# A transformer block of eight sequences: the hand-written step orders of five stages are replaced

## The reference

```python
x = layernorm(x + attention(x))      # 16 heads of 16, Wqkv, bqkv, Wo, bo
x = layernorm(x + ffn(x))            # expert width 1024
```

## Time and profile before

| | |
|---|---|
| median of 3 runs | 621.63 us (621.22 to 622.06) |
| profiled execution, its span | 619.31 us |
| TensorE matmul, busy | 583.6 us, 94% |
| VectorE, busy | 494.4 us, 80% |
| ScalarE, busy | 318.8 us, 51% |
| GpSimd, busy | 299.0 us, 48% |
| mean share of the DMA engines | 37.5% |

### The profile page before, as it was taken

How to read it: one execution, slowest core, us unless ns; L and a number is a source line. 1 busy time by engine, 2 the same in 40 slices (tenths; PEclk the granted TensorE clock), 3 DMA queues, 4 the chain that set the end, 5 groups by cost and what they waited for, 6 DMA issues and landing times.

```text
span 619.3 us, 12888 instructions
## 1 busy us (share of the span) xinstructions
PE 583.6 (94%) x4012; PEld 342.5 (55%) x4012; DVE 494.4 (80%) x1258; ACT 318.8 (51%) x593; POOL 299.0 (48%) x504
## 2 busy tenths in 40 slices
PE   5789888999999999999999999999999999999995
PEld 3344354664656555674556646575556646446674
DVE  5388968996799868989599877989599877993766
ACT  2129713459247644477246653476345753576262
POOL 1306695346275535465174543654264452654234
PEclk9789998999999999999999999999999999999998
DMA  6965715005462073502653064601644054600101
GB/s 158 289 175 206 211 51 161 23 29 163 122 172 66 3 229 115 166 1 83 161 166 100 1 199 123 160 28 52 186 144 127 1 166 105 206 2 3 35 1 35
DMA packets 47724, 68.49 MB, mean 111 GB/s; under 512 B 4857, under 2 KB 43641, under 8 KB 44793
## 3 DMA queue, kind: packets, MB, share of 16 engines
q1 hardware_dynamic: 47691, 68.08, 37.5%
HBM read 38.44 MB, written 29.36 MB: 109 GB/s over the span
## 4 chain that ended last, share of the span: by engine, by line
PE 78%; DVE 5%; ACT 5%; POOL 5%; issue 4%; DMA 2%; SPq 0%; POOLq 0%; DVEq 0%
PE ring L698 17%; PE max_bank L613 10%; PE acc L647 9%; PE ring L635 9%; PE ring L590 8%; PE acc L715 7%; PE ring L597 4%; ACT probs L772 4%; PE ring L671 4%; PE max_bank L618 2%; PE ring L655 2%; POOL probs L1042 2%; PE ring L684 1%; POOL tern_down L1085 1%; PE max_bank L715 1%
## 5 line engine op out<-in xcount | busy, mean ns | idle before, releaser
L772 ACT ACTIVATE probs<-ring 128x512 f32<-128x512 f32 x320 | 170.7, 606 | 45.6 <-PE ring L635 44.0
L1042 POOL TENSOR_SCALAR_AFFINE_SELECT probs<-probs 128x256 f32<-128x256 f32 (+1 forms) x320 | 120.5, 401 | 130.1 <-ACT probs L772 129.4
L896 DVE CUSTOM_DVE_ANT_0 max_bank<-max_bank,causal_wide 128x384 f32<-128x384 f32 (+1 forms) x256 | 157.2, 637 | 15.3 <-PE max_bank L613 12.2
L613 PE MATMUL max_bank<-k_stack,q_stack 112*128 112x384 bf16 (+3 forms) x512 | 123.4, 304 | 5.9 <-DVE neg_max L896 2.8
L1078 POOL TENSOR_TENSOR hidden_lo<-hidden,hidden_hi 128x512 f16<-128x512 f32 (+1 forms) x72 | 75.1, 1050 | 63.6 <-ACT hidden_hi L803 63.3
L635 PE MATMUL ring<-q_stack,k_stack 114*128 114x512 bf16 (+3 forms) x512 | 103.7, 300 | 1.6 <-DVE attn L921 0.5
L791 ACT ACTIVATE gating<-ring,tanh_scale 128x512 f32<-128x512 f32 (+1 forms) x72 | 45.8, 639 | 74.0 <-PE ring L698 74.0
L647 PE MATMUL acc<-probs,v_ones 128*32 128x512 f32 (+3 forms) x1024 | 79.9, 437 | 2.8 <-POOL probs L1042 2.8
L613 PEld LDWEIGHTS max_bank<-k_stack,q_stack 112*128 112x128 bf16 x512 | 46.5, 98 | 54.0 <-DVE neg_max L896 15.3
L900 DVE TENSOR_REDUCE neg_max<-max_bank 128x2 f32<-128x512 f32 (+1 forms) x96 | 63.7, 686 | 10.4 <-PE max_bank L618 8.7
L635 PEld LDWEIGHTS ring<-q_stack,k_stack 114*128 114x128 bf16 x512 | 44.5, 97 | 49.4 <-issue 17.0
(11 more groups left out here) (107 smaller groups left out, 866.0 us busy)
## 6 DMA issues: line engine op xcount, KB each, us to landing
q_stack<-qk_scratch SPq DMA_DIRECT2D x15, 768.0 KB, 6.1
k_stack<-k_slots SPq DMA_DIRECT2D x15, 768.0 KB, 7.8
qk_scratch<-qk_parts SPq DMA_DIRECT2D x16, 384.0 KB, 3.0
k_slots<-qk_parts SPq DMA_DIRECT2D x16, 384.0 KB, 2.6
xin<-x_dram SPq DMA_DIRECT2D x8, 512.0 KB, 3.5
qk_scratch<-qk_parts SPq DMA_DIRECT2D x16, 256.0 KB, 3.2
k_slots<-qk_parts SPq DMA_DIRECT2D x16, 256.0 KB, 2.3
res<-x_dram SPq DMA_DIRECT2D x8, 512.0 KB, 3.4
```

The source lines that it names most:

```text
L613: mm = pe.matmul(max_bank[k][:, width * i:width * (i + 1)], q_stack[0:MAX_ROW, 4 * g + h, P * tile:P * (tile + 1)], k_stack[0:MAX_ROW, 4 * ...
L772: rg.drained(act.activation(probs[:, g % 2, n, :], rg.bank(step)[:, :], ACT.Exp), step)
L896: dve.tensor_tensor_reduce(scores, scores, causal_wide[:, SEQ - width:SEQ], -1.0, LOWEST_START, ALU.add, ALU.min, neg_max[:, g, first_col: ...
L1042: return pool.affine_select(out=v, in_=v, compare_op=ALU.is_ge, fill=0.0, base=0, pattern=([[0, blocks]] if blocks > 1 else []) + [[1, P]] ...
```

## The change

The order strings of FIRST, SECOND, LOOP, SEVENTH and LAST are written anew; PRE's is as it was. Every string holds the same steps as before (217, 261, 261, 245 and 110), so no operation is added, removed or given to another engine. The wait that VectorE did in SEVENTH before overwriting `z` is now done in every stage but FIRST.

What moves, in the main:

- LOOP, TensorE: the front was qk.2, max.0.0, max.0.1, qk.3, v.0, max.0.2, x1t.0, ... and is v.0, max.0.0, v.1, max.0.1, qk.2, qk.3, max.0.2, max.0.3, x1t.0, ... The up and gate steps come earlier in part; qk.0 and qk.1 come one exp later each at the end.
- LOOP, VectorE: ln2 goes from behind mt_out.3 to directly in front of wo.0.1; nt_out.1 from before split.1 to behind the copy of pv.2.3; ffn_stats.1 behind mt_out.3; ln1 behind take.0.0.
- LOOP, GpSimd and SyncE: on GpSimd load_res's four additions go from before split.2 to behind hidden_hi.2. On SyncE load_next and load_res go in front of part_write.3.2 and stack_read.1, and store from before part_write.0.1 to behind stack_read.0. 
- SECOND: four v and qk.2, qk.3 in front of x1t.0 (before: three v, both qk); ln1 behind take.0.9 (before: take.0.7); ln2 at the end as in LOOP; load_next first and load_res in the middle.
- SEVENTH: v.1 and qk.3 come in front of x1t.0, pv and exp steps earlier, load_res late, and the store before the last pv steps.
- FIRST: v.0 in front of qk.3, wsum behind exp.2.6 (before: exp.3.3), qk.0 before max.3.0 and ternary.1 in front of the copy of pv.2.3, nt_out.1 behind it; at.0 between pv.3.0 and pv.3.1.
- LAST: another order in the middle; gate.7.1 before down.2.1, ln2.0 before ffn_sum.1.

```diff
--- before.py
+++ after.py
...
 FIRST_ORDER = """
-    qk.2 qk.3 part_write.2.0 v.0 split.2 max.0.0 max.0.1 max.0.2 max.0.3 max.0.4 max.0.5 max.0.6 part_write.3.0
-    take.0.0 max.0.7 max.0.8 take.0.1 take.0.2 max.0.9 take.0.3 take.0.4 v.1 max.0.10 max.1.0 take.0.5 take.0.6
...
-    pv.1.1 nt.0 exp.2.6 take.3.10 mt.3 qk.1 exp.2.7 split.0 exp.2.8 mt_out.3 exp.2.9 pv.1.2 nt_out.0 pv.1.3 exp.3.0
-    exp.3.1 part_write.0.1 exp.3.2 exp.3.3 qk_out.1 nt.1 split.1 wsum exp.3.4 exp.3.5 exp.3.6 exp.3.7 nt_out.1
-    exp.3.8 pv.2.0 exp.3.9 pv.2.1 ternary.0 ternary.2.0 pv.2.2 pv.2.3 nt.2 ternary.2.1 pv.3.0 part_write.0.2 pv.3.1
-    pv.3.2 part_write.1.0 ternary.1 part_write.1.1 part_write.1.2 nt_out.2 pv.3.3 at.0 ternary.2.2 nt.3 nt_out.3
-    wo.0.0 wo.1.0 at.1 wo.0.1 stack_read.0 wo.1.1
+    split.2 take.0.0 qk.2 v.0 take.0.1 qk.3 max.0.0 v.1 take.0.2 max.0.1 take.0.3 take.0.4 max.0.2 max.0.3 max.0.4
+    max.0.5 max.0.6 max.0.7 max.0.8 split.3 take.0.5 take.0.6 part_write.2.0 part_write.2.1 take.0.7 max.0.9
...
+    exp.2.5 split.0 take.3.10 nt_out.0 mt.3 exp.2.6 mt_out.3 wsum part_write.1.0 exp.2.7 part_write.1.1 exp.2.8
+    pv.1.2 part_write.1.2 exp.2.9 ternary.0 qk.1 exp.3.0 part_write.0.2 pv.1.3 exp.3.1 exp.3.2 exp.3.3 exp.3.4
+    exp.3.5 exp.3.6 nt.1 exp.3.7 stack_read.0 qk_out.1 exp.3.8 split.1 pv.2.0 exp.3.9 pv.2.1 ternary.2.0 pv.2.2
+    ternary.2.1 ternary.1 pv.2.3 nt.2 pv.3.0 at.0 nt_out.1 pv.3.1 nt_out.2 pv.3.2 pv.3.3 wo.0.0 nt.3 nt_out.3 at.1
+    wo.1.0 wo.0.1 wo.1.1 ternary.2.2
...
 SECOND_ORDER = """
-    max.0.0 v.0 max.0.1 v_out.0 qk.2 take.0.0 max.0.2 max.0.3 take.0.1 take.0.2 max.0.4 max.0.5 v.1 take.0.3 max.0.6
-    take.0.4 take.0.5 take.0.6 max.0.7 qk.3 v.2 take.0.7 ln1 max.0.8 v_out.1 max.0.9 load_next x1t.0 x1t.1 take.0.8
-    split.2 x1_lo.0 max.0.10 x1_lo.1 take.0.9 v_out.2 up.0 part_write.2.0 up.1 part_write.2.1 max.1.0 gate.0
...
-    ffn_stats.0 exp.3.0 exp.3.1 ffn_stats.1 exp.3.2 exp.3.3 pv.2.0 exp.3.4 exp.3.5 nt_out.0 exp.3.6 exp.3.7 exp.3.8
-    pv.2.1 pv.2.2 pv.2.3 exp.3.9 nt.1 ln2 nt.2 nt_out.1 pv.3.0 load_res pv.3.1 pv.3.2 part_write.1.2 nt_out.2 pv.3.3
-    at.0 nt.3 wo.0.0 nt_out.3 at.1 stack_read.0 store wo.1.0 wo.0.1 wo.1.1
+    take.0.0 load_next take.0.1 max.0.0 max.0.1 qk.2 v.0 v.1 take.0.2 v.2 v_out.0 take.0.3 v_out.1 take.0.4 max.0.2
+    max.0.3 v_out.2 take.0.5 take.0.6 take.0.7 v_out.3 max.0.4 take.0.8 max.0.5 take.0.9 max.0.6 ln1 take.0.10
+    max.0.7 max.0.8 take.1.0 x1_lo.0 max.0.9 v.3 qk.3 max.0.10 max.1.0 x1t.0 x1t.1 part_write.3.0 max.1.1 x1_lo.1
...
+    ffn_stats.0 exp.3.4 pv.2.0 exp.3.5 exp.3.6 part_write.1.0 nt_out.0 split.1 exp.3.7 exp.3.8 part_write.0.2 pv.2.1
+    pv.2.2 pv.2.3 nt_out.1 exp.3.9 part_write.1.1 part_write.1.2 nt.1 nt.2 nt_out.2 pv.3.0 pv.3.1 pv.3.2
+    stack_read.0 store ffn_stats.1 pv.3.3 at.0 nt.3 nt_out.3 wo.0.0 at.1 ln2 wo.1.0 wo.0.1 wo.1.1
...
 LOOP_ORDER = """
-    qk.2 max.0.0 max.0.1 take.0.0 qk.3 take.0.1 v.0 max.0.2 ln1 x1t.0 max.0.3 x1t.1 max.0.4 v.1 v_out.0 take.0.2
-    load_res take.0.3 max.0.5 v.2 part_write.3.0 max.0.6 max.0.7 x1_lo.0 take.0.4 take.0.5 part_write.2.0 x1_lo.1
-    v_out.1 v_out.2 split.2 up.0 take.0.6 take.0.7 gate.0 swish.0 max.0.8 up.1 swiglu.0 split.3 take.0.8
...
-    max.1.7 down.1 swiglu.3 v.3 take.1.5 hidden_hi.3 swiglu.4 max.1.8 max.1.9 v_out.3 gate.5 take.1.6 hidden_hi.4
-    part_write.3.2 up.6 max.1.10 stack_read.1 take.1.7 up.7 max.2.0 mt_out.0 exp.0.0 swish.5 take.1.8 max.2.1
-    swiglu.5 load_next down.2 take.1.9 max.2.2 take.1.10 exp.0.1 swish.6 max.2.3 take.2.0 take.2.1 exp.0.2 swish.7
...
-    mt_out.3 qk.0 exp.2.8 nt.0 ln2 exp.2.9 qk_out.0 pv.1.2 part_write.0.0 pv.1.3 nt_out.0 exp.3.0 exp.3.1 store
-    split.0 exp.3.2 qk.1 exp.3.3 part_write.0.1 exp.3.4 nt.1 exp.3.5 qk_out.1 exp.3.6 exp.3.7 exp.3.8 nt_out.1
-    exp.3.9 pv.2.0 split.1 pv.2.1 pv.2.2 pv.2.3 pv.3.0 nt.2 part_write.1.0 part_write.0.2 pv.3.1 pv.3.2
-    part_write.1.1 nt_out.2 pv.3.3 at.0 nt.3 nt_out.3 part_write.1.2 wo.0.0 at.1 wo.1.0 wo.0.1 wo.1.1 stack_read.0
+    take.0.0 v.0 v_out.0 ln1 max.0.0 v.1 split.2 part_write.3.0 v_out.1 part_write.2.0 take.0.1 take.0.2
+    part_write.2.1 max.0.1 take.0.3 qk.2 qk.3 take.0.4 x1_lo.0 x1_lo.1 max.0.2 max.0.3 x1t.0 max.0.4 take.0.5
+    take.0.6 swish.0 take.0.7 swiglu.0 part_write.2.2 x1t.1 v_out.2 max.0.5 swish.1 v.2 take.0.8 split.3 max.0.6
...
+    down.1 mt.0 hidden_hi.1 v_out.3 max.1.5 gate.4 swish.3 max.1.6 max.1.7 hidden_hi.2 take.1.1 swiglu.2 up.5
+    max.1.8 gate.5 load_res max.1.9 hidden_hi.3 up.6 swish.4 part_write.3.2 stack_read.1 max.1.10 take.1.2 down.2
...
+    nt.0 ffn_stats.1 exp.2.8 nt_out.0 qk.0 exp.2.9 pv.1.2 exp.3.0 pv.1.3 exp.3.1 qk_out.0 exp.3.2 exp.3.3 qk.1
+    part_write.0.0 exp.3.4 exp.3.5 split.0 qk_out.1 part_write.0.1 exp.3.6 exp.3.7 exp.3.8 nt.1 exp.3.9 split.1
+    pv.2.0 part_write.0.2 part_write.1.0 pv.2.1 pv.2.2 part_write.1.1 pv.2.3 nt_out.1 pv.3.0 nt.2 pv.3.1 pv.3.2
+    part_write.1.2 nt_out.2 pv.3.3 nt_out.3 at.0 ln2 stack_read.0 nt.3 wo.0.0 at.1 wo.1.0 wo.0.1 wo.1.1 store
...
 SEVENTH_ORDER = """
-    qk.2 max.0.0 max.0.1 v.0 v_out.0 max.0.2 take.0.0 take.0.1 max.0.3 ln1 load_res take.0.2 x1t.0 v.1 split.2
-    max.0.4 x1t.1 max.0.5 v_out.1 take.0.3 x1_lo.0 qk.3 take.0.4 part_write.3.0 max.0.6 take.0.5 max.0.7 x1_lo.1 v.2
...
-    ffn_stats.0 ffn_sum.1 pv.2.3 pv.3.0 ffn_stats.1 pv.3.1 pv.3.2 pv.3.3 nt.2 nt_out.2 nt.3 at.0 nt_out.3 at.1 ln2
-    wo.0.0 wo.0.1 store wo.1.0 wo.1.1
+    take.0.0 part_write.3.0 v_out.0 part_write.2.0 take.0.1 qk.2 max.0.0 part_write.2.1 max.0.1 v.0 ln1 take.0.2
+    v_out.1 v.1 take.0.3 take.0.4 max.0.2 max.0.3 take.0.5 qk.3 part_write.2.2 max.0.4 take.0.6 x1_lo.0 x1t.0
+    max.0.5 max.0.6 x1_lo.1 x1t.1 max.0.7 take.0.7 take.0.8 split.2 part_write.3.1 v.2 v_out.2 max.0.8 take.0.9 up.0
...
+    exp.3.9 pv.2.0 pv.2.1 ffn_stats.1 pv.2.2 pv.2.3 pv.3.0 pv.3.1 pv.3.2 pv.3.3 nt_out.2 nt.2 nt.3 at.0 nt_out.3 ln2
+    at.1 wo.0.0 wo.0.1 wo.1.0 wo.1.1
...
 LAST_ORDER = """
-    ln1.0 x1t.0 x1_lo.0 up.0.0 swish.0.0 up.1.0 swish.1.0 gate.0.0 up.2.0 ln1.1 swiglu.0.0 swish.2.0 gate.1.0
...
-    swiglu.7.1 down.5.1 down.6.1 hidden_hi.7.1 down.7.1 ffn_sum.1 ffn_stats.1 ln2.0 ln2.1 store.0 store.1
+    x1t.0 ln1.0 x1_lo.0 up.0.0 swish.0.0 gate.0.0 swiglu.0.0 swish.1.0 swiglu.1.0 swish.2.0 swish.3.0 up.1.0
...
+    swiglu.7.1 gate.7.1 down.2.1 ln2.0 down.3.1 down.4.1 down.5.1 ffn_sum.1 ffn_stats.1 down.6.1 ln2.1 down.7.1
...
@@ -927,8 +927,8 @@
                         u = step[1]
                         bank = ("wo", u, 0)
                         if u == 0:
-                            if name == "SEVENTH":
-                                dve.wait_ge(y_done, TT * b)
+                            if not first:
+                                at_least(dve, y_done, TT, b, 0)
                                 dve.sem_inc(dve_passed, 1)
                             at_least(dve, res_biased, 1, b, 1)
                         rg.wait_filled(dve, bank)
```

116 lines of the change are left out of this document (58 added, 58 removed).

## The result

The changed kernel took 632.75 us (median of 4 runs, 630.98 to 633.23), the kernel before 621.73 us (4 runs, 621.22 to 622.06). The ratio is 1.0183, with a 95% interval of 1.0163 to 1.0204: the change made the kernel 11 us slower. The profiled execution spans 631.40 us, 12.1 more than that of before.

The account below looks back on a forecast made before the run. TensorE, busy 94% of the span, was taken as the bound. Terms -0.5 - 2.0 - 2.0 - 1.4 - 0.4 = -6.3 us took the span from 619.31 to 613.0; adding 2.32 gave 615.3, range 609 to 624.

Parts of the forecast that it names:

- What changes is cover: All stages: a new order changes only the TensorE work standing between a chain's start and the step needing its end.
- 5 x -0.4: LOOP's term: five iterations each 0.4 us shorter, -2.0 us in all; bounds per iteration -0.7 and +1.0.
- The 0.4 us goes: LOOP: with qk.1 one exp later, pv.3.0's 0.4 us wait for GpSimd's mask disappears.
- The sums of TensorE's work up to pv.2.0 and behind it come out the same.: LOOP: the new order leaves TensorE's total work on either side of pv.2.0 unchanged.
- The slack that I summed: LOOP: least slack of VectorE's takes against TensorE's max steps, first 10 us, goes from -0.2 to +0.3.
- -2.0: SECOND's term: x1t wait -1.5, takes -0.4, slow clock -0.1; bounds -4 and +3.5 us.
- the second rival: LOOP stays and var_eps meets GpSimd's step, making SECOND +1.0 instead of -2.0: 620.3 us; chance 0.20.
- -1.4: SEVENTH's term: more TensorE work ahead of x1t.0 removes the 1.37 us lost there; bounds +0.5 and -2.5.
- tight place further on: SEVENTH's upper bound: another tight place later in the stage could make it 0.5 us longer.
- -0.5: FIRST's term: copy 2.3 us later, way behind it 2.0 shorter, 0.8 of VectorE's front idle gone; bounds -5.5, +8.
- The third's event: FIRST: GpSimd takes the port first and holds VectorE's ternary.1 for 5.4 to 10.8 us; middle 623.4, chance 0.15.
- The first's: FIRST pays in full, 5.5 us gained instead of 0.5, total 610.3 us; chance 0.13.

Follow-up runs that it names:

- c3: Kernel before with GpSimd's third down-weight instruction moved behind split.3 in SECOND, and LOOP's nt.1, nt_out.1, ln2 and store moved as in the change: 616.93 us, ratio 0.9933.
- b2: Changed kernel with FIRST as before, SECOND's qk.3 behind v.2, LOOP's nt.1 and nt_out.1 earlier, SEVENTH's down.3 ahead of exp.3.0: 629.23 us, ratio 1.0118.
- b1: Kernel before with SECOND as changed but qk.3 behind v.2, and LOOP's qk.0 and qk.1 one exp later each: 624.86 us, ratio 1.0051.
- a2: Changed kernel with LOOP's pv.1.0 put directly ahead of pv.1.1 and pv.1.2 directly ahead of pv.1.3: 635.57 us, ratio 1.0206.
- b3: Changed kernel with FIRST's ternary.1 behind the copy and nt_out.1 ahead, LOOP's pv groups joined at the earlier place, SEVENTH as before: 642.97 us, ratio 1.0333.
- a4: Changed kernel with SECOND's qk.3 directly behind v.2 instead of behind v.3: 630.40 us, ratio 1.0139.
- c1: Changed kernel with LOOP as before, SECOND's qk.3 behind v.2, SEVENTH's down.3 ahead of exp.3.0, FIRST's v.1 and v.2 later: 625.31 us, ratio 1.0085.
- d1: Changed kernel with LOOP as before, SECOND's qk.3 behind v.2, SEVENTH's down.3 ahead of exp.3.0, FIRST's mt.1 behind max.2.3: 624.56 us, ratio 1.0034.
- a3: Changed kernel with GpSimd's third down-weight instruction moved from the end of FIRST to SECOND, behind split.2: 632.50 us, ratio 1.0142.
- e1: As d1, but FIRST in the old order up to max.2.0 and in the changed order from there: 621.90 us, ratio 1.0017.

## Why the prediction was wrong, by its steps

The forecast span was 613.0, the measured one 631.4. Of the 18.4 us between, PRE, which had no term, makes 2.6, by chance. The step that failed in the four stages below is the same one, "What changes is cover": cover was followed only to the wait that each move was meant for, and what the moved step itself sets off, or had covered until then, was counted as nothing.

**LOOP (5 x -0.4; measured 5 x +0.7; 5.7 us of the miss).** "The 0.4 us goes" was right as an event and wrong in its cause. It is nt_out.1 behind the copy that frees pv.3.0 (c3, and b2 the other way), not the later qk steps: without it, both of them one exp later cost 0.84 (b1), and pv.3.0 still waited. What failed is the sentence before: "The sums of TensorE's work up to pv.2.0 and behind it come out the same." They don't, because a pv group costs 0.09 to 0.11 us to enter and 0.12 to 0.14 to leave wherever no other wait stands there, and the new order has two groups more (about 0.46 us); and because a bank four steps back is not read out yet when TensorE does three exps in 0.66 us (exp.3.7, 0.36 instead of 0.10). pv.3.0 gave 0.54 back; some 0.2 at the front and 0.3 around qk.0 and qk.1 came on top. Joining groups did not pay (a2, b3), so the price of a group is read from starts and not from a run that is faster by it. The slack that I summed was for takes only, not for banks that ScalarE or qk_out drains. The Trainium skill (TensorEngine Tiling (Array Packing), Key Properties) says that changing the tiling mode drains TensorE; pv is the one step with 32 columns in these rows, and the prices at its edges fit that, though no run here tells a drain from another cause. ln2 was hidden as forecast, and the reads caused no wait.

**SECOND (-2.0; measured +1.86; 3.9 us).** The wait of x1t went, as forecast. I set all four v and both qk ahead of x1t and did not follow qk.3 on: its place behind v.3 delays split.3, part_write and the read of the key stack, which max.2.0 awaits. (The row max.0.2 to max.0.9 is 1.6 us by its own prices, not 1.5, which changes nothing.) That place of qk.3 cost 2.9 to 3.8 us (a4, c1, d1) and turned a gain into a loss. The block of var_eps came as the second rival had it (3.06 us), but it moved SECOND's end by 1.0 us in this order (a3) and by 0.2 to 0.3 with qk.3 early (c1 and d1 against a4).

**SEVENTH (-1.4; measured +1.38; 2.8 us).** x1t no longer waits for ln1, but the forecast 1.4 was not won: VectorE comes as late to its takes as it came to ln1, and TensorE now waits there, 0.77 us in starts at max.0.4 and 0.43 at max.0.6, against 1.35 in front of x1t.0 before:

```profile
534.04 0.34 PE L613 MATMUL max_bank<-k_stack,q_stack 112*128 112x384 bf16 x1 [0.60 <-DVE neg_max L900]
...
535.25 0.34 PE L613 MATMUL max_bank<-k_stack,q_stack 112*128 112x384 bf16 x1 [0.27 <-DVE neg_max L896]
```

So x1t.0 started 7.4 us after the stage's start and not 6.6. The "tight place further on" was sized at +0.5 and is 1.6: exp.3.0 is late by 1.08 for the landing of the maxima of quad 3, which have only down.0 to down.2 and two exps to cover their way to the query stack, and mt.3, which transposes them, by 0.51. With down.3 there as well, b2 got 0.98 back.

**FIRST (-0.5; measured +2.18; 2.7 us).** By parts, before and after:

| us | start to max.2.0 | to max.3.10 | to exp.3.9 | to the copy's end | to FIRST's end |
|---|---|---|---|---|---|
| before | 23.06 | 18.60 | 12.16 | 2.58 | 10.70 |
| after | 25.07 | 19.76 | 11.19 | 3.33 | 9.93 |

In the forecast's own terms: the front was to gain 0.8, counted up to VectorE's last take, and lost 3.2; from there to the copy's end 2.3 were to be added, and 13.18 us instead of 13.41 are 0.2 less; behind the copy 2.0 were to go, and 0.8 went. The front, up to the end of the last take, before and after:

```profile
18.96:61.95 42.99, 38.00 (x201) 18.01 (x203) 31.70 (x86) 20.46 (x39) 16.83 (x35) 0.89 0.68 212
```

```profile
21.51:67.68 46.17, 39.89 (x209) 18.54 (x207) 33.94 (x90) 22.78 (x40) 17.54 (x35) 0.87 0.69 210
```

VectorE does 2.2 us more work there: split.0's four instructions now stand ahead of the last take. The forecast left that out, and left the same 2.2 in the way to the copy, where it is gone. Its idle time, of which 0.8 was to go, grew by 0.9 instead: that is the failed part of the front. On TensorE the loss lies in the first part, up to max.2.0 (2.0 us); the second part holds two pv steps more now, and with the third it takes 30.95 us instead of 30.76. In seven profiles with the old first part it took 21.1 to 24.9, in nine with the new one 24.5 to 26.6. Behind the copy, 9.93 instead of the forecast 8.7, since nt.2 waits for nt_out.1's bank, 0.7 us that my list left out (the other 0.5 is open); and 2.3 us more are handed to SECOND, where VectorE is free at 6.00 instead of 3.72. The granted clock takes a share: from 5 to 38 us after FIRST's start its mean was 0.90 before and 0.84 after (first row before, second after):

```profile
23.96:56.96 33.00, 28.05 (x150) 13.76 (x152) 26.59 (x70) 14.88 (x29) 13.12 (x27) 0.90 0.69 219
```

```profile
26.51:59.51 33.00, 27.21 (x135) 13.29 (x134) 26.13 (x67) 13.40 (x26) 12.58 (x25) 0.84 0.73 227
```

Over all profiles the old order had 0.84 to 1.00 there, the new one 0.74 to 0.84. Ahead of each fall in FIRST's front TensorE does maxima at the pace of the takes. b2 has the old order and the mean clock of the new one:

```profile
26.61:59.61 33.00, 28.60 (x141) 14.52 (x139) 26.04 (x69) 13.35 (x27) 11.47 (x24) 0.84 0.65 209
```

It took 55.5 us to exp.3.9, where before took 53.8 and the changed order 56.0. From this one profile an estimate is that 1.7 of the 2.2 us go with the clock and 0.5 with the order itself. Which steps of the new front bring the lower clock, or whether a part of it is chance, stays open: v.1, v.2 and mt.1 do not bring it, each by one profile (c1, d1).

**LAST (-0.4; measured +0.39)** can't be told from chance. **The rivals:** of the second, var_eps met GpSimd's step as it said, but at a small price; LOOP did not stay, it grew, and SECOND's loss came from qk.3. The third's event did not occur in the changed kernel; b3 shows it to be real, in an order with ternary.1 behind the copy. The first's did not occur.

## What to carry to other kernels

A step moved ahead to cover one wait has to be followed along everything that hangs on it: qk.3's DMA chain, the bank four steps on, the next reader of the same port. Where the bounding engine hardly idles (0.58 of 71.38 us here), compare the starts of its steps and not its idle time: switches between forms and short bank waits hide in "busy". A scattered step can be cover for its neighbours; joining such steps pays only where something else covers the same waits. And a stage's time in one profile can move by several us without any change of the stage (PRE, and FIRST's old order), so a small difference needs medians or several profiles.

## What the runs showed of the hardware

Entering a group of 32-column matmuls cost 0.09 to 0.11 us and leaving it 0.12 to 0.14, in SECOND, LOOP and SEVENTH of both kernels, wherever no other wait stood. A VectorE instruction of 4 elements a partition can stand 3.06 us behind a GpSimd instruction that started before it, and one of 2048 elements took 5.60 instead of 1.31. The same order of PRE took 12.7 to 16.8 us in sixteen executions: qk.0 waited for the landing of its weights for 1.11 us in e1 and 2.77 in a3, and from its start to that of qk.1 passed 1.79 us at the upper level of TensorE's clock (before, e1) and 3.4 at the lower (0.50 granted; the changed kernel, a3).
